# Second normalisation of a conv and graph-attention block: four slices of variances on rows of their own

## The chip, the cores and the metric

The kernel runs on one core of a Trainium2 chip. The metric is the device time of one launch in microseconds; lower is better.

## What is computed

The input x is 16 images of 64 channels, 56 x 56 pixels, in f32. The reference does, cut to what matters:

```
x = x + conv3x3(bfp8(_ln_c(x)), bfp8(weight)) + bias     # _ln_c: over channels
t = tokens of x                                          # 16*3136 tokens of 64 channels
t = t + ffn(_ln_t(t))        # _ln_t: (t - mean) / sqrt(var + 1e-5), over the 64 channels
# ffn: h = t @ W_gat (16 numbers a token); graph attention over 262144 edges + loops;
#      the sums choose 2 of 4 experts per token; each expert is 64 -> 128 -> gelu -> 64
```

The change lies in `_ln_t`, the second normalisation.

## The kernel before, in words

The program has three phases, one behind the other, with a barrier between them.

The first phase counts and ranks the edges, normalises x the first time, quantises it, convolves it, normalises the sum the second time (`D`, the tokens) and projects the tokens. Beside that it sorts the edges: 32 groups of edges (`SG`) each give a table `run_slots`, which GpSimd scatters to memory with 17 indirect DMAs a group (line 470, 544 in all). The second phase gathers node rows by edge, 16 gathers a step (line 1097), adds up the attention sums and runs the experts. The third phase weighs and adds the experts' outputs.

There is no scheduler: each engine has its own program, in the order written, and waits on semaphores.

An image lies in SBUF as 128 partitions (two halves of the rows, 64 channels each) by 4 chunks of 392 pixels. A loop over image pairs (`image_pair`) handles image `b` on each engine as follows.

- VectorE: one-hot tables for the sort (lines 837, 839), the sum of convolution and input (line 972), `spread_step` (844), the rest of the one-hots, the centring `D = X - mean` (981), one more `spread_step`, then the reciprocal of `std2` (986), the product `D * rstd` (988) and the places of the group (851 to 860).
- ScalarE: squares of `D` into `S` (707), the root of the variances into `std2` (709), the copy of the sort's sums into `run_slots` (`group_out`, 669), the copy of the projected rows (701).
- TensorE: the mean (`mean_of`, 530), half a sort step (16 matmuls, 582), the variances (637), half a sort step, the spreading of the reciprocals (643), half a sort step, then, once line 988 is done, the convolution of the next image (614), half a sort step and the projection (623).
- GpSimd: the 17 scatters of a group, once `slots` (860) and `run_slots` (669) of that group are there. The two buffers of `run_slots` are filled again when their scatters have landed.
- SyncE: loads of images, stores of `X`, `D` and `rows`, and at the end waits for all stores.

The variances: for chunk `c` a 128 x 32 matrix `thin` (1/64 in column 0 for the upper half's channels, in column 1 for the lower half's) is the stationary operand, the 392 squares of the chunk are moved, and the result lies in rows 32c and 32c+1 of PSUM tile `A`, 392 columns wide. Root and reciprocal work on 128 x 392, though two rows in 32 hold something. `fan` (32 rows of a chunk by 128) then spreads each chunk's two rows over 64 partitions each.

In the compiled program an f32 matmul is two pairs of a weight load and a matmul (two passes), standing one behind the other; the profile counts both. The four matmuls of line 637 write four column strips of 32 of the array (`128*32` in the profile); the four of line 643 read four row strips of 32 (`32*128`).

Of the kernel before, what the change touches and what calls it, by code (L numbers as in the profile page):

```python
# [11 lines left out]
ALU = mybir.AluOpType  # L12
ACT = mybir.ActivationFunctionType
AX = mybir.AxisListType

P = 128


B, CH, HGT, WID = 16, 64, 56, 56
# [3 lines left out]
CHUNK = HALF // CHUNKS  # L23
# [18 lines left out]
FLAT_P = GROUPS_P * GROUP  # L42
assert QCHUNKS * QGROUPS == GROUPS_P
QUAD = P // CHUNKS
MAGIC = 1.5 * 2.0 ** 23
TINY = 2.0 ** -100
EXP_BITS = 0x7F800000
# [75 lines left out]
def link(eng, instr, sig):  # L123

    instr.then_inc(sig.sem, 1)
    sig.k += 1
    eng.wait_ge(sig.sem, sig.value)
# [19 lines left out]
def build(nc, x, conv_w, conv_b, w_gat, att_src, att_dst, b_gat, ln_g, ln_b, w1, b1, w2, b2, edges, out):  # L147
    ctx = ExitStack()
    with ctx:
        def sb(name, shape, dt=F32):  # L150
            return ctx.enter_context(nc.sbuf_tensor(name, shape, dt))
# [31 lines left out]
        eps_t = sb("eps_t", [P, 1])  # L183
# [11 lines left out]
        b2s = sb("b2s", [P, EXPERTS])  # L195
        pick = sb("pick", [2 * 3 * EXPERTS, EXPERTS, P], BF16)
        fold = sb("fold", [P, CH])
        thin = sb("thin", [P, QUAD])
        fan = sb("fan", [P, P])

        A = ctx.enter_context(nc.psum_tensor("A", [P, 4, 512], F32))
        C = ctx.enter_context(nc.psum_tensor("C", [P, 4, 512], F32))

        with ExitStack() as ph:
            def tb(name, shape, dt=F32):
                return ph.enter_context(nc.sbuf_tensor(name, shape, dt))
# [12 lines left out]
                t.append(edge_t[:].bitcast(F32)[:, 0:HALF].rearrange("p (c n) -> p c n", c=CHUNKS))  # L219
            S = tb("S", [P, CHUNKS, CHUNK])  # L220
            Q = [tb(f"Q{k}", [P, HALF_ROWS + 2, WID + 2], BF16) for k in range(2)]
            std2 = tb("std2", [P, CHUNK])
            dev = tb("dev", [TOK, TOK_TILES, 2])
            rstd = tb("rstd", [TOK, TOK_TILES, 2])
            rows = tb("rows", [TOK, TOK_TILES, 2 * ROW])
# [180 lines left out]
            def _(pool):  # L406
                step = Signal(s["pstep"])
                link(pool, pool.memset(tally[:], 0.0), step)
                for r in range(2):
# [3 lines left out]
                                              pattern=[[-1, P]], channel_multiplier=1), step)  # L413
# [3 lines left out]
                for r in range(2):  # L417
                    link(pool, pool.affine_select(out=fold[:], in_=fold[:], compare_op=ALU.not_equal, fill=1.0, base=-r * CH,
                                                  pattern=[[-1, CH]], channel_multiplier=1), step)
# [3 lines left out]
                                              pattern=[[-1, P]], channel_multiplier=1), step)  # L423
# [6 lines left out]
                for h in range(2):  # L430
                    link(pool, pool.memset(halves[h * CH:(h + 1) * CH, h * CH:(h + 1) * CH], 1.0 / CH), step)
                link(pool, pool.memset(thin[:], 0.0), step)
                for h in range(2):
                    link(pool, pool.memset(thin[h * CH:(h + 1) * CH, h:h + 1], 1.0 / CH), step)
                link(pool, pool.memset(fan[:], 0.0), step)
                for c in range(CHUNKS):
                    for h in range(2):
                        link(pool, pool.affine_select(out=fan[:, h * CH:(h + 1) * CH], in_=fan[:, h * CH:(h + 1) * CH], compare_op=ALU.not_equal, fill=1.0,
                                                      base=-(c * QUAD + h), pattern=[[0, CH]], channel_multiplier=1), step)
                link(pool, pool.memset(eps_c[:], 1e-6), step)  # L440
                link(pool, pool.memset(eps_t[:], 1e-5), step)
                for k in range(2):
# [9 lines left out]
                for h in range(2):  # L452
                    mine = pick[:, :, h * CH:(h + 1) * CH]
                    for r in range(3):
                        link(pool, pool.affine_select(out=mine, in_=mine, compare_op=ALU.not_equal, fill=1.0, base=-(h * 3 + r) * EXPERTS,
                                                      pattern=[[-1, EXPERTS], [0, CH]], channel_multiplier=1), step)
                pool.memset(scratch_i[:], 0).then_inc(s["const_ready"], 1)

                n = PLACES * RUN * FIELDS // 8
# [92 lines left out]
            def _(pe):  # L552
                pe.wait_ge(s["rank_const"], 2)
                for b in range(NB):
                    pe.wait_ge(s["masks_ready"], b + 1)
                    for c in range(4):
                        mm = pe.matmul(C[:, c, :], tally[:, TWIN - 1 - b:TWIN - 1 - b + P], mask_h[:, b % 2, c * PSUM_COLS:(c + 1) * PSUM_COLS],
                                       start=(b == 0), stop=(b == NB - 1))
# [4 lines left out]
                n = NB * SG // 4  # L563
# [63 lines left out]
                def image_pair(i, last=False):  # L627
                    for k in range(2):
                        b, g = i * 2 + k, i * 2 + k + SG // 2 + 1
                        sorts = not (last and k == 1)  # L630
                        pe.wait_ge(s["summed"], b + 1)
                        mean_of(pe, X[k], s["mean2_ready"])
                        if sorts:
                            sort_step(g, 1 - k, 0, 0)
                        pe.wait_ge(s["squared2"], b + 1)
                        for c in range(CHUNKS):
                            mm = pe.matmul(A[c * QUAD:(c + 1) * QUAD, 0, 0:CHUNK], thin[:], S[:, c, :], start=True, stop=True)
                        mm.then_inc(s["var2_ready"], 1)
                        if sorts:
                            sort_step(g, 1 - k, 0, 1)  # L640
                        pe.wait_ge(s["rstd2_ready"], b + 1)
                        for c in range(CHUNKS):
                            mm = pe.matmul(A[:, c, 0:CHUNK], fan[c * QUAD:(c + 1) * QUAD, :], std2[c * QUAD:(c + 1) * QUAD, :], start=True, stop=True)
                        mm.then_inc(s["rstd2_spread"], 1)
                        if sorts:
                            sort_step(g, 1 - k, 1, 0)
                        pe.wait_ge(s["tokens_ready"], b + 1)
                        if sorts:
                            convolve(i + k, 1 - k)
                            sort_step(g, 1 - k, 1, 1)  # L650
                        project(b, k)
# [6 lines left out]
            @block.scalar  # L658
            def _(act):
                act.wait_ge(s["const_ready"], 1)  # L660
                act.wait_ge(s["blocks_ready"], 1)
                act.dma_start(blk_d.rearrange("(p k) -> p k", p=P), unit_blk_i[:]).then_inc(s["blk_stored"], 16)

                def group_out(i, k):

                    act.wait_ge(s["step_sums"], i * 4 + k * 2 + 2)
                    if not (isinstance(i, int) and i == 0):
                        act.wait_ge(sent[k], i * (RUN_COLS * 16))
                    act.copy(run_slots[:, k].rearrange("p c v -> p v c"),  # L669
                             C[:, k, 0:FIELDS * SLOT_COLS].rearrange("p (v c) -> p v c", v=FIELDS)).then_inc(s["group_out"], 1)  # L670

                def deviations(eps, k, ready):
                    act.activation(dev[:].rearrange("p j h -> p (j h)"), C[0:TOK, k, VAR_AT:VAR_AT + 2 * TOK_TILES], ACT.Sqrt, bias=eps[0:TOK]).then_inc(ready, 1)

                def part_squares(u):
                    b, k, cs, part = part_of(u)
                    act.wait_ge(s["centred"], u + 1)
                    act.activation(S[:, cs], D[k][:, cs], ACT.Square).then_inc(s["squared"], 1)

                def part_deviations(u):  # L680
                    b, k, cs, part = part_of(u)
                    act.wait_ge(s["var_ready"], u + 1)
                    act.activation(dev1[:, part].rearrange("p j h -> p (j h)"), A[0:PTOK, cs.start, CHUNK:CHUNK + 2 * PTOK_TILES], ACT.Sqrt,
                                   bias=eps_c[0:PTOK]).then_inc(s["deviated"], 1)

                part_squares(0)
                for u in range(UNITS):
                    part_deviations(u)
                    if u + 1 < UNITS:
                        part_squares(u + 1)  # L690
                for k in range(2):
                    group_out(0, k)
                with act.Fori(1, SG // 4) as i:
                    for k in range(2):
                        group_out(i, k)
                group_out(SG // 4, 0)
                def rows_out(b):
                    act.wait_ge(s["projected"], b + 1)
                    if not (isinstance(b, int) and b == 0):
                        act.wait_ge(s["rows_stored"], b * 32)  # L700
                    act.copy(rows[:].rearrange("p (k j) f -> p k (j f)", k=2), C[0:TOK, 2:4, 0:14 * ROW]).then_inc(s["rows_ready"], 1)

                def image_pair(i, last=False):
                    for k in range(2):
                        b = i * 2 + k
                        act.wait_ge(s["centred2"], b + 1)
                        act.activation(S[:], D[k], ACT.Square).then_inc(s["squared2"], 1)
                        act.wait_ge(s["var2_ready"], b + 1)
                        act.activation(std2[:], A[:, 0, 0:CHUNK], ACT.Sqrt, bias=eps_t[:]).then_inc(s["deviated2"], 1)
                        if not (last and k == 1):  # L710
                            group_out(i + SG // 4 + k, 1 - k)
                        rows_out(b)
                image_pair(0)
                with act.Fori(1, B // 2 - 1) as i:
                    image_pair(i)
                image_pair(B // 2 - 1, True)

            @block.vector
# [958 lines left out]
```

## Time and profile before

| what | value |
|---|---|
| median of three runs | 4388.38 us (4383.29 to 4395.43) |
| the profiled execution | 4386.45 us, its span 4384.7 us |
| VectorE busy | 2789.1 us, 64% |
| GpSimd busy | 2963.9 us, 68% |
| TensorE busy | 3496.4 us, 80%; granted clock 0.806 on average |
| ScalarE busy | 1013.6 us, 23% |

The first phase lies at 0 to about 1291 us of the span, the second at 1292 to about 4064, the third behind it. The images of the second normalisation come at 870 to 1287 us. A row of the profile names the line, the engine, the tiles written and read and the time; in brackets stand the idle time before it and who ended it.

### The profile page before, as it was taken

How to read it: one execution, taken by the hardware profiler on the slowest of the kernel's cores; microseconds unless marked ns; L12 is line 12 of the kernel's file. 1: busy time of each engine (PE TensorE's matmuls, PEld its weight loads, DVE VectorE, ACT ScalarE, POOL GpSimd, SP SyncE). 2: the span in 40 equal slices, each digit the busy share in tenths (PEclk: the TensorE clock that was granted, in tenths of full speed). 3: DMA queues.
4: the chain of work that ended last, by engine and by line, in shares of the span. 5: the costliest groups of instructions: out<-in, count | busy, mean ns of one | idle time of the engine just before them, and what ended most of it. 6: DMA issues, size and time to landing. Idle time of an engine off the chain costs nothing. (4 is left out here: it accounts for less than half of the span.)

```text
span 4384.7 us, 60136 instructions
## 1 busy us (share of the span) xinstructions
PE 3496.4 (80%) x19024; PEld 2414.3 (55%) x19025; DVE 2789.1 (64%) x3513; ACT 1013.6 (23%) x1820; POOL 2963.9 (68%) x2936
## 2 busy tenths in 40 slices
PE   4786333488853999999999999999999999986064
PEld 1454323355543766676676667666666666666010
DVE  8788999888864455455455545554545454545977
ACT  0110000011111333333333333333333333320100
POOL 3000788887757777777777777777777777776088
PEclk8898555688875899889889988988988898887555
DMA  1243111399989222222222222222222222221299
GB/s 51 60 103 84 43 48 48 48 116 115 122 114 86 37 38 34 37 37 37 33 37 37 34 36 37 37 33 33 37 34 36 33 37 36 35 27 10 93 301 340
DMA packets 357672, 284.59 MB, mean 65 GB/s; under 512 B 253586, under 2 KB 329938, under 8 KB 357204
## 3 DMA queue, kind: packets, MB, share of 16 engines
q1 hardware_dynamic: 245620, 199.65, 22.1%
q0 software_dynamic: 87552, 29.20, 7.2%
q10 hardware_dynamic: 24416, 54.71, 6.0%
q8 instruction: 42, 0.69, 0.1%
q14 instruction: 42, 0.34, 0.0%
HBM read 161.06 MB, written 122.27 MB: 65 GB/s over the span
## 5 line engine op out<-in xcount | busy, mean ns | idle before, releaser
L1097 POOL DMA_INDIRECT gath<-tab_d,src_no x2116 | 1996.6, 944 | 644.9 <-issue 644.9
L470 POOL DMA_INDIRECT edge_d<-run_slots,slots x544 | 672.9, 1237 | 569.4 <-ACT run_slots L669 406.6
L1401 DVE TENSOR_TENSOR acc<-acc,C 128x160 f32 x1090 | 349.8, 321 | 1043.8 <-PE C L1228 930.9
L1228 PEld LDWEIGHTS C<-spread,lo_hot 128*128 128x128 f32 x4360 | 776.9, 236 | 257.9 <-issue 194.7
L1228 PE MATMUL C<-spread,lo_hot 128*128 128x160 f32 x4360 | 846.4, 360 | 72.9 <-DVE spread L1389 71.0
L1212 PEld LDWEIGHTS C<-damp,lo_hot_t 128*128 128x128 f32 x4384 | 558.6, 207 | 85.6 <-issue 85.6
L1212 PE MATMUL C<-damp,lo_hot_t 128*128 x4384 | 575.5, 288 | 5.8 <-ACT lo_hot_t L1125 5.8
L1139 ACT ACTIVATE mlp<-A,b2s 64x392 f32<-64x392 f32 x512 | 298.0, 582 | 1068.8 <-PE A L1247 1068.8
L1237 PE MATMUL A<-T,w1s 64*128 64x392 f32 x1024 | 525.7, 596 | 23.4 <-DMA T<-t_d 23.4
L582 PE MATMUL C<-wide_rec,hot_lo 128*128 128x136 f16 x2048 | 271.7, 305 | 298.0 <-DVE wide_rec L844 298.0
L1247 PE MATMUL A<-hid,w2s 128*64 128x392 f32 x1024 | 451.8, 523 | 0.0
L582 PEld LDWEIGHTS C<-wide_rec,hot_lo 128*128 128x128 f16 x2048 | 241.8, 123 | 350.1 <-DVE wide_rec L844 292.0
L1130 ACT ACTIVATE hid<-A,b1s 128x392 f32<-128x392 f32 x512 | 300.6, 587 | 483.7 <-PE A L1237 483.6
L1389 DVE TENSOR_TENSOR spread<-hi_hot,C 128x2560 f32<-128x2560 f32 x137 | 386.4, 2820 | 4.7
L1125 ACT COPY lo_hot_t<-A 128x512 f32<-128x512 f32 x548 | 292.8, 588 | 235.7 <-PE A L1202 235.7
L1202 PEld LDWEIGHTS A<-ident,lo_hot 128*128 128x128 f32 x2192 | 241.3, 143 | 192.2 <-issue 192.1
L1202 PE MATMUL A<-ident,lo_hot 128*128 128x128 f32 x2192 | 303.3, 282 | 41.0 <-PE A L1237 35.3
L1329 DVE TENSOR_TENSOR lo_hot<-C,lo 128x2048 f32<-128x2048 f32 x137 | 314.0, 2292 | 16.3
L1237 PEld LDWEIGHTS A<-T,w1s 64*128 64x128 f32 x1024 | 165.1, 201 | 268.9 <-issue 238.7
L669 ACT CAST run_slots<-C 128x136 f16<-128x136 f32 x32 | 10.0, 312 | 677.4 <-PE C L582 615.6
L1379 DVE TENSOR_TENSOR C<-gath,C 128x64 f32<-128x64 f32 x137 | 31.3, 229 | 210.9 <-DMA gath<-tab_d,src_no 184.8
L1576 POOL TENSOR_TENSOR four<-pairs 128x392 f32<-128x392 f32 x64 | 79.1, 1235 | 127.6 <-DVE pairs L1654 126.3
(272 smaller groups left out, 3247.0 us busy)
## 6 DMA issues: line engine op xcount, KB each, us to landing
mlp_d<-mlp ACTq DMA_DIRECT2D x128, 392.0 KB
mlp<-mlp_d SPq DMA_DIRECT2D x64, 784.0 KB, 6.5
gath<-tab_d,src_no POOLq DMA_INDIRECT x2116
pixels<-in_x SPq DMA_DIRECT2D x32, 392.0 KB, 6.4
src<-in_x SPq DMA_DIRECT2D x32, 392.0 KB, 6.5
T<-t_d SPq DMA_DIRECT2D x128, 98.0 KB
X<-x_d SPq DMA_DIRECT2D x64, 196.0 KB, 8.4
out<-X SPq DMA_DIRECT2D x128, 98.0 KB, 6.8
```

The lines of the kernel that those rows point to most:

```text
L470: pool.indirect_dma_start(edge_d, bass.IndirectOffsetOnAxis(ap=slots[:, k, c:c + 1], axis=0), run_slots[:, k, c * RUN:(c + 1) * RUN, :].re ...
L582: mm = pe.matmul(C[:, k, 0:FIELDS * SLOT_COLS], hot_lo[:, j, t // LINE, :, t % LINE], fields[:, t // LINE, :, t % LINE], start=(j == 0 and ...
L1097: pool.indirect_dma_start(gath[:, g % BUFS, j, :], None, node_d if g < BUFS else tab_d, bass.IndirectOffsetOnAxis(ap=src_no[:, t:t + 1], a ...
L1130: act.activation(hid[:], A[:, 2, 0:CHUNK], ACT.Gelu, bias=b1s[:, e:e + 1]).then_inc(s["gelu_ready"], 1)
L1202: mm = pe.transpose(A[:, j // 4, (j % 4) * P:(j % 4 + 1) * P], lo_hot[:, k, half * G // 2 + j, :], ident[:])
L1212: mm = pe.matmul(C[:, 0, t * HI * HEADS:(t + 1) * HI * HEADS], lo_hot_t[:, t, :], damp[:, bass.ds(qs[t // U - half * UG // 2], HI), :].rea ...
L1228: mm = pe.matmul(C[:, bank, at:at + HI * VALS], lo_hot[:, k % UNROLL, u * U + j, :], spread[:, u * U + j].rearrange("p h v -> p (h v)"), s ...
L1237: pe.matmul(A[:, 2, 0:CHUNK], w1s[a, e, :], T[a, :], start=True, stop=True).then_inc(s["hidden"], 1)
L1247: pe.matmul(A[h * CH:(h + 1) * CH, 3, 0:CHUNK], w2s[:, e, :], hid[:], start=True, stop=True).then_inc(s["expert_done"], 1)
L1329: dve.tensor_tensor(lo_hot[:, k], lane_v.rearrange("p (k h) -> p k h", k=1).broadcast_to([P, G, P]), lo[:, bass.ds(g * G, G)].rearrange("p ...
L1389: dve.tensor_tensor(spread[:], hi_hot[:, k].rearrange("p t (h k) -> p t h k", k=1).broadcast_to([P, G, HI, VALS]), vals.rearrange("p t (k ...
L1401: L(dve.tensor_tensor(here, here, C[:, bank, at:at + HI * VALS].rearrange("p (h v) -> p h v", h=HI), ALU.add))
```

## The change

A chunk's 392 pixels are cut into four slices of 98. The variances of slice n go to rows 32c + 2n and 32c + 2n + 1, so all four slices of a chunk share the same 98 columns, and `std2` is 128 x 98. For that `thin` and `fan` have four versions, one a slice; each of the four matmuls of line 637 becomes four that add into the same 32 x 98 of PSUM (the columns of `thin` that aren't slice n's are zero), and each of the four of line 643 becomes four of 98 columns.

```
-        thin = sb("thin", [P, QUAD])
-        fan = sb("fan", [P, P])
+        thin = sb("thin", [P, SLICES, QUAD])
+        fan = sb("fan", [P, SLICES, P])
...
-            std2 = tb("std2", [P, CHUNK])
+            std2 = tb("std2", [P, SLICE])
...
-                for h in range(2):
-                    link(pool, pool.memset(thin[h * CH:(h + 1) * CH, h:h + 1], 1.0 / CH), step)
+                for n in range(SLICES):
+                    for h in range(2):
+                        link(pool, pool.memset(thin[h * CH:(h + 1) * CH, n, 2 * n + h:2 * n + h + 1], 1.0 / CH), step)
                 link(pool, pool.memset(fan[:], 0.0), step)
                 for c in range(CHUNKS):
                     for h in range(2):
-                        link(pool, pool.affine_select(out=fan[:, h * CH:(h + 1) * CH], in_=fan[:, h * CH:(h + 1) * CH], compare_op=ALU.not_equal, fill=1.0,
-                                                      base=-(c * QUAD + h), pattern=[[0, CH]], channel_multiplier=1), step)
+                        mine = fan[:, :, h * CH:(h + 1) * CH]
+                        link(pool, pool.affine_select(out=mine, in_=mine, compare_op=ALU.not_equal, fill=1.0,
+                                                      base=-(c * QUAD + h), pattern=[[-2, SLICES], [0, CH]], channel_multiplier=1), step)
...
                         for c in range(CHUNKS):
-                            mm = pe.matmul(A[c * QUAD:(c + 1) * QUAD, 0, 0:CHUNK], thin[:], S[:, c, :], start=True, stop=True)
+                            for n in range(SLICES):
+                                mm = pe.matmul(A[c * QUAD:(c + 1) * QUAD, 0, 0:SLICE], thin[:, n, :], S[:, c, n * SLICE:(n + 1) * SLICE],
+                                               start=(n == 0), stop=(n == SLICES - 1))
...
                         for c in range(CHUNKS):
-                            mm = pe.matmul(A[:, c, 0:CHUNK], fan[c * QUAD:(c + 1) * QUAD, :], std2[c * QUAD:(c + 1) * QUAD, :], start=True, stop=True)
+                            for n in range(SLICES):
+                                mm = pe.matmul(A[:, c, n * SLICE:(n + 1) * SLICE], fan[c * QUAD:(c + 1) * QUAD, n, :], std2[c * QUAD:(c + 1) * QUAD, :],
+                                               start=True, stop=True)
...
-                        act.activation(std2[:], A[:, 0, 0:CHUNK], ACT.Sqrt, bias=eps_t[:]).then_inc(s["deviated2"], 1)
+                        act.activation(std2[:], A[:, 0, 0:SLICE], ACT.Sqrt, bias=eps_t[:]).then_inc(s["deviated2"], 1)
```

## Rows read from the trace of the kernel before

**Rows 1.** Groups of GpSimd at 1310 to 4060 us: busy, mean ns, idle before and releasers

```profile
L1097 POOL DMA_INDIRECT gath<-tab_d,src_no x2116 | 1996.6, 944 | 644.9 <-issue 644.9
```

**Rows 2.** Groups of GpSimd at 902 to 1252 us

```profile
L470 POOL DMA_INDIRECT edge_d<-run_slots,slots x230 | 281.2, 1223 | 70.1 <-issue 68.0 <-ACT run_slots L669 1.8 <-DVE slots L860 0.3
```

**Rows 3.** Timeline of the end of the first phase: start us, us, instruction, [idle before]

```profile
1261.68 0.96 POOL L470 DMA_INDIRECT edge_d<-run_slots,slots  x1 [0.31 <-issue]
1263.84 0.31 ACT L669 CAST run_slots<-C 128x136 f16<-128x136 f32 x1 [14.80 <-PE C L582]
1264.94 0.96 POOL L470 DMA_INDIRECT edge_d<-run_slots,slots  x1 [2.30 <-ACT run_slots L669]
...
1285.13 0.96 POOL L470 DMA_INDIRECT edge_d<-run_slots,slots  x1 [0.31 <-issue]
1285.94 0.72 ACT L701 COPY rows<-C 112x672 f32<-112x672 f32 x1 [11.79 <-PE C L623]
1286.75 1.11 SPq L377 DMA_DIRECT2D node_d<-rows  x2
...
1292.04 1.11 SPq L1068 DMA_DIRECT2D lo_hot<-edge_d  x2
```

**Rows 4.** Waits of SyncE's queue at 1280 to 1300 us: total, times, longest

```profile
SPq L401 <- DMA node_d<-rows: 3.2, 1, 3.2
```

**Rows 5.** Timeline of one image's normalisation, from the squares to the convolution

```profile
1032.58 1.51 ACT L707 ACTIVATE S<-pixels 128x1568 f32<-128x1568 f32 x1 [4.26 <-DVE pixels L981]
1033.90 2.50 DVE L844 TENSOR_TENSOR wide_rec<-flat_count,rec 128x2176 f16<-128x2176 f16 x2 [0.16 <-DVE flat_count L839]
1034.14 0.96 PE L637 MATMUL A<-S,thin 128*32 128x392 f32 x8 [1.95 <-ACT S L707]
1035.04 2.19 PE L582 MATMUL C<-wide_rec,hot_lo 128*128 128x136 f16 x16
1035.15 0.59 ACT L709 ACTIVATE std<-A,eps_t 128x392 f32<-128x392 f32 x1 [1.06 <-PE A L637]
1036.31 2.60 DVE L986 RECIPROCAL std<-std 128x392 f32<-128x392 f32 x1
1038.96 1.69 PE L643 MATMUL A<-std,fan 32*128 32x392 f32 x8 [1.74 <-DVE std L986]
1040.72 1.79 DVE L988 TENSOR_TENSOR pixels<-pixels,A 128x1568 f32<-128x1568 f32 x1 [1.81 <-PE A L643]
```

**Rows 6.** Groups of VectorE at 902 to 1252 us

```profile
L986 DVE RECIPROCAL std<-std 128x392 f32<-128x392 f32 x14 | 36.4, 2600 | 0.1
L988 DVE TENSOR_TENSOR dst<-dst,A 128x1568 f32<-128x1568 f32 x7 | 12.5, 1789 | 11.2 <-PE A L643 11.2
L988 DVE TENSOR_TENSOR pixels<-pixels,A 128x1568 f32<-128x1568 f32 x6 | 10.7, 1788 | 10.1 <-PE A L643 10.1
```

**Rows 7.** Smaller operations of the same kinds, from the groups by form

```profile
L915 DVE RECIPROCAL rstd<-dev 98x16 f32<-98x16 f32 x32 | 7.9, 246 | 5.2 <-ACT dev L683 5.2
L683 ACT ACTIVATE dev<-A,eps_c 98x16 f32<-98x16 f32 x32 | 8.8, 274 | 235.9 <-PE A L496 235.9
```

**Rows 8.** TensorE started by 1007.75 us, and the granted clock (next to last group) in four bursts

```profile
1007.70 0.88 PE L637 MATMUL A<-S,thin 128*32 128x392 f32 x4 [2.09 <-ACT S L707]
...
1034.09:1035.10 1.01, 0.96 (x9) 0.23 (x10) 1.01 (x1) 0.00 (x0) 0.70 (x2) 0.84 1.37 208
1038.90:1040.70 1.80, 1.74 (x9) 0.63 (x10) 0.01 (x1) 0.00 (x0) 1.50 (x2) 0.50 0.04 2
1007.65:1009.30 1.65, 1.60 (x10) 0.34 (x11) 1.65 (x2) 0.00 (x0) 1.35 (x2) 0.50 1.28 257
1012.50:1013.60 1.10, 1.01 (x10) 0.46 (x11) 0.04 (x2) 0.00 (x0) 0.88 (x1) 1.00 0.03 2
```

**Rows 9.** Timeline of TensorE: f32 bursts in column strips and on the whole array

```profile
204.28 1.57 PE L507 MATMUL A<-ident,rstd 98*64 98x98 f32 x32
...
1024.61 2.88 PE L623 MATMUL C<-proj,dst 128*112 128x48 f32 x28
```

**Rows 10.** Timeline of the constants: GpSimd, then VectorE's masks beside them and alone

```profile
2.90 0.62 POOL L418 TENSOR_SCALAR_AFFINE_SELECT fold<-fold 128x64 f32<-128x64 f32 x2
7.73 8.56 POOL L438 TENSOR_SCALAR_AFFINE_SELECT fan<-fan 128x64 f32<-128x64 f32 x8
17.50 6.30 DVE L742 TENSOR_SCALAR mask_h<-blk_h 128x2048 bf16<-128x2048 bf16 x4
35.79 0.71 POOL L457 MEMSET scratch_i<- 128x128 int32 x1
53.04 0.69 DVE L742 TENSOR_SCALAR mask_h<-blk_h 128x2048 bf16<-128x2048 bf16 x1 [0.23 <-PE C L557]
68.55 2.29 DVE L746 TENSOR_REDUCE group_tot<-C 128x32 f32<-128x2048 f32 x1 [1.13 <-PE C L557]
```

More of the change, by code:

```diff
@@ L44 @@
 QUAD = P // CHUNKS
+SLICES = 4
+SLICE = CHUNK // SLICES
+assert SLICE * SLICES == CHUNK and 2 * SLICES <= QUAD
 MAGIC = 1.5 * 2.0 ** 23
```

## The prediction, made before the changed kernel ran

> **What bounds the kernel now.** I read the page's slices first, then the groups of GpSimd by stage, then the timeline of one image and of the end of the first phase.
>
> The second phase is GpSimd's: 2116 gathers are busy 1996.6 us and sit idle 644.9 us for nothing but their own issue [rows 1]. It starts when the first phase ends, so what the change does to the end of the first phase reaches the total one for one, and nothing else of it does.
>
> In the stage that the change touches, GpSimd is full too. In 350 us it made 230 scatters, 281.2 us busy and 68.0 us issue; it waited 2.1 us for others [rows 2]. So 17 scatters, a group, take 350 / 230 x 17 = 25.9 us. A lone scatter takes 0.96 us and 0.30 to issue [rows 3], 21.4 us a group; the other 4 us are scatters that last longer than 0.96 us (the mean is 1.22) and that come whatever the reciprocal does.
>
> VectorE keeps nearly the same pace beside it: there is almost no idle time but 21.3 us in 13 images ahead of line 988, waiting for line 643 [rows 6]. So two chains run side by side. How they end is in [rows 3]: GpSimd's scatter of 1261.68 ends at 1262.64, and the last group's first waits for ScalarE's copy until 1264.94, that is 2.0 us beyond its normal 0.30. Its seventeenth ends at 1286.09. The image chain ends with the rows' copy at 1286.66 and their store at 1286.75; SyncE waits 3.2 us for that store alone [rows 4], and issues the next phase's first load at 1292.04. SyncE came to that wait from the one on GpSimd's block at about 1288.0 (1291.2 less 3.2, where 1291.2 is the end of the wait as I read it, 0.8 us ahead of the next phase), so the scatters had landed 3.9 us before the rows' store at most (at 1287.3 if a scatter lands 1.2 us behind its row).
>
> **The change, part by part.** *The reciprocal.* 16 columns take 246 ns [rows 7] and 392 take 2600 [rows 6]: 6.26 ns a column, so 98 take 246 + 82 x 6.26 = 759 ns. It saves 1.84 us an image, 29.4 us over 16. *The root.* 274 ns at 16 columns [rows 7], 590 at 392 [rows 5]: 98 take 343, 0.25 us saved, on the chain only if the root is late.
>
> *The matmuls.* Columns moved stay the same, instructions go from 8 to 32 passes a burst. What a pass of 98 columns costs is in line 507: 32 passes in two column strips side by side, 1.57 us with about 0.22 of tail, so 16 after one another in a strip, 84 ns each [rows 9]; the loads of 64 columns are covered. Line 623 shows a pass that its weight load bounds: 28 in 2.88 us, 103 ns for 112 columns [rows 9]; the new `fan` passes load 128, so I take 103 x 128 / 112 = 118 ns. Both at the clock's upper level; at the lower one twice that.
>
> How many passes lie side by side is what decides. Before, line 637 had four of its eight passes started within 50 ns (x4) [rows 8], though in the program the second pass of strip 0 stands ahead of the first of strip 1. So TensorE lets a strip's instructions wait and starts those behind them for another strip, at least 6 instructions further on (second load and pass of three strips). For full overlap it has to reach past 14 waiting ones of each of three strips, 42. The trace shows no such reach, nor that it fails.
> - Full overlap: 8 passes deep, 0.67 us and 0.94 us, with tails of about 0.2: T1 = 0.9, T2 = 1.15, sum 2.05; at the lower clock 3.8 us.
> - No overlap: 32 x 84 ns = 2.7 and 32 x 118 = 3.8, with tails 6.9 us; at the lower clock 13.
> - A reach of 4 to 8 instructions a strip: the next strip starts when 5 (or 3) passes of this one have run, 3 x 5 + 8 = 23 (or 17) deep: 1.9 + 2.7 + 0.4 = 5.0 (or 3.8) us; lower clock twice.
>
> The Trainium skill, "TensorE: Matmul & The Clock Gate", section on packing small matmuls, says that matmuls start and end strictly in program order. By it the first strip's eight passes would run ahead of the second's, the row "no overlap". The x4 row speaks against it in its strict form.
>
> *What these cost the image.* The squares end at 1034.09 and line 988 starts at 1040.72, 6.6 us later; VectorE is free for the reciprocal 2.25 us after the squares, then 2.6 and 1.64 us of mean wait (21.3 / 13) give 6.5 as the mean [rows 5, 6]. Afterwards TensorE sets it: T1, half a sort step 2.17 us that stands between the bursts, T2, and 0.25 us of hand-overs; the reciprocal is done before. So line 988 comes at T1 + T2 + 2.4, and the **break-even is T1 + T2 = 4.1 us**. VectorE's spare time isn't lost otherwise: the convolution follows 988, and conv, sort half, projection and mean stand in the same order as before. So d = 4.1 - (T1 + T2) is gained, or lost, an image.
>
> *What reaches the end.* A gain ends where GpSimd does: the 3.9 us by which it was ahead, and the 2.0 us that its last group waited, 5.9 us. 16 d reaches that at d = 0.37, so T1 + T2 = 3.75 is enough, which full overlap gives even at the lower clock. A loss has no such cover: ScalarE's copy of the last group comes 15 d later, the last rows 16 d. Line 637 and 643 together saw both clock levels (0.50, 0.50, 0.84, 1.00) [rows 8].
>
> *Constants.* Eight `affine_select` of 256 columns for 64: 0.24 us in line 418 [rows 10], I estimate 0.14 more each, 1.1 us; six more small memsets and two wider ones 1.3 us. They end at 36.5 us, VectorE needs them at 68 [rows 10]: 30 us of cover. But VectorE's masks take 6.30 / 4 = 1.58 us beside GpSimd's work and 0.69 + 0.23 alone [rows 10], so 2.4 us more of it cost up to 2.4 x 0.42 = 1.0 us ahead of everything. Between 0 and 1.0 I take 0.5. If GpSimd slows as in line 438 (0.94 us a select for 0.24), this could be three times as much.
>
> **The sum.** -5.9 + 0.5 = -5.4 us for full overlap: the profiled execution goes from 4386.45 to 4381.05; the median of the runs is 1.93 above it, so 4388.4 - 5.4 = **4383 us**. 0.3% of this kernel, 13 us, is what a measurement can tell from no change.
>
> **Rivals.**
> - *A, the forecast*: overlap deep enough, GpSimd bounds. 4383, own range 4377 to 4391. For it: strips overlap already, and the cap makes the result insensitive. 47%.
> - *B, strips one after another (ends slower)*: line 637 and 643 fill one strip's queue and the others stand idle. Place: the two bursts between squares and line 988; d = 4.1 - 6.9 = -2.8, x 16 = 45 us, 4433; nearer 4480 with half of it at the lower clock. It decides from T1 + T2 above 4.9 (13 us). For it: all passes of a strip now follow one another. Against it: the x4 row. 20%. The rule of the Trainium skill's "TensorE: Matmul & The Clock Gate" would give this rival.
> - *C, a short reach*: 3.8 to 5.0 us at the upper clock, half as much again with mixed clocks, 5.7 to 7.5: d from +0.3 to -3.4, times between 4384 and 4440, the middle 4405. 28%, of which a quarter stays within 13 us of before.
> - *D, all of the reciprocal reaches the end*: 4388 - 29 = 4359. It needs GpSimd to get faster by 25 us, which the 2.1 us of waits exclude unless its long scatters shrink. 3%.
> - *E, the change is lost in something else*, such as more instructions to fetch, within 13 us: 2%.
>
> Faster by over 0.3%: D, 3%. Same: A, a quarter of C, E: 56%. Slower: the rest of C and B, 41%. The range goes from 4376 to 4432: left out are D, and of B and C what mixed clocks make longer, some 17%.
>
> **What would show it.** Line 986 at 0.76 us and line 709 at 0.34. Line 637 and 643 with 32 passes each in 0.9 and 1.2 us (A), in 2 and 2.7 (C), 2.7 and 3.8 (B). In A the wait ahead of GpSimd's last group is gone and SyncE's last wait is for the scatters; in B and C line 988 waits 3 us and more, and the last group's wait grows by 15 d. The prediction is wrong if TensorE's reach is short, or if the longer bursts run at the lower clock where the reach is middling.

## The result, and the profile after

The changed kernel takes 4414.05 us (median of 5 runs, 4404.73 to 4420.42) where the kernel before takes 4393.65 us (median of 5 runs, the three of the table above among them). The ratio is 1.0048, 95% interval 1.0029 to 1.0067: slower, by 13 to 29 us. Forecast was 5.4 us less than before. Three single runs in this document (one of the kernel before, two of later experiments) took 4630 to 5496 us at a granted clock of 0.58 to 0.72 over the whole run, and are left out of every median, count and ratio below. The profiled execution took 4407.87 us, its span is 4406.1 us, 21.4 us more than before's.

The small operations are as forecast. Groups of VectorE in the stage of the images (busy us, mean ns, idle time ahead and who ended it), to be read beside [rows 6]:

```profile
L997 DVE TENSOR_TENSOR pixels<-pixels,A 128x1568 f32<-128x1568 f32 x8 | 14.3, 1788 | 29.7 <-PE A L651 29.7
L997 DVE TENSOR_TENSOR dst<-dst,A 128x1568 f32<-128x1568 f32 x7 | 12.5, 1787 | 25.2 <-PE A L651 25.2
L995 DVE RECIPROCAL std<-std 128x98 f32<-128x98 f32 x16 | 12.3, 767 | 6.3 <-ACT std L718 4.8
```

The reciprocal (now line 995) fell from 2600 to 767 ns; 759 was forecast. But the product behind it (988 before, 997 now) waits (29.7 + 25.2) / 15 = 3.66 us for TensorE's spreading matmuls, where it waited 21.3 / 13 = 1.64 us. One image shows why; this is the stretch of [rows 5] in the new kernel:

```profile
1012.41 1.51 ACT L716 ACTIVATE S<-dst 128x1568 f32<-128x1568 f32 x1 [3.79 <-DVE dst L990]
1013.74 2.49 DVE L853 TENSOR_TENSOR wide_rec<-flat_count,rec 128x2176 f16<-128x2176 f16 x2 [0.16 <-DVE flat_count L848]
1013.97 1.97 PE L643 MATMUL A<-S,thin 128*32 128x98 f32 x32 [1.49 <-ACT S L716]
1015.88 2.16 PE L587 MATMUL C<-wide_rec,hot_lo 128*128 128x136 f16 x16
1015.99 0.34 ACT L718 ACTIVATE std<-A,eps_t 128x98 f32<-128x98 f32 x1 [2.06 <-PE A L643]
1016.36 0.77 DVE L995 RECIPROCAL std<-std 128x98 f32<-128x98 f32 x1
1017.97 2.72 PE L651 MATMUL A<-std,fan 32*128 32x98 f32 x32
1020.73 1.79 DVE L997 TENSOR_TENSOR dst<-dst,A 128x1568 f32<-128x1568 f32 x1 [3.60 <-PE A L651]
```

The variances (now line 643) take 1.97 us and the spreading (now 651) 2.72 us, both at the clock's upper level:

```profile
1013.90:1015.95 2.05, 1.98 (x33) 1.83 (x34) 2.05 (x2) 0.02 (x1) 1.66 (x2) 1.00 1.23 275
1017.90:1020.70 2.80, 2.80 (x35) 2.63 (x34) 0.00 (x0) 0.00 (x0) 2.19 (x3) 1.00 0.05 3
```

(Windows: stretch, length, then busy time of TensorE, its weight load, VectorE, ScalarE, GpSimd, then the granted clock, here 1.00, the share of the DMA engines and GB/s.) So the reciprocal is done at 1017.13, 0.8 us before TensorE comes out of its half sort step and can use it, and the 2.72 us behind it are all on the path. The sum of the two bursts is 4.69 us against the break-even of 4.1.

The end of the first phase, as in [rows 3]:

```profile
1278.09 0.31 ACT L678 CAST run_slots<-C 128x136 f16<-128x136 f32 x1 [16.07 <-PE C L587]
1279.20 0.96 POOL L475 DMA_INDIRECT edge_d<-run_slots,slots  x1 [3.06 <-ACT run_slots L678]
...
1300.87 0.72 ACT L710 COPY rows<-C 112x672 f32<-112x672 f32 x1 [11.63 <-PE C L628]
1301.68 1.10 SPq L380 DMA_DIRECT2D node_d<-rows  x2
1306.95 1.10 SPq L1077 DMA_DIRECT2D lo_hot<-edge_d  x2
```

The wait ahead of GpSimd's last group did not go, it grew from 2.30 to 3.06 us. GpSimd's waits for `run_slots` over the whole stage (total us, times, longest) show more, first before and then after the change:

```profile
POOL edge_d L470 <- ACT run_slots L669: 4.4, 8, 2.3
```

```profile
POOL edge_d L475 <- ACT run_slots L678: 12.0, 11, 3.1
```

So GpSimd, which was nearly always busy or issuing before, is now held up by the image chain ahead of several of its last groups. The next phase starts at 1306.95 instead of 1292.04, 14.9 us later. The images themselves begin 3.1 us later. Here is the first convolution in each kernel, before and after:

```profile
852.28 2.14 PE L614 MATMUL A<-Q,cw_t 128*128 128x392 bf16 x6 [2.62 <-DMA pixels<-in_x]
```

```profile
855.42 1.81 PE L619 MATMUL A<-Q,cw_t 128*128 128x392 bf16 x5 [3.65 <-DMA pixels<-in_x]
```

From there to the store of the last rows it is 1286.75 - 852.28 = 434.5 us before and 1301.68 - 855.42 = 446.3 after: **the image chain is 11.8 us longer**. The rest of the 21.4 us is 3.1 us ahead of it, and 6.5 us in the second and third phases, where the kernels are the same: their gathers end 5.4 us further apart (2737.0 us from the first gather to the last, 2731.6 before). A second execution of the changed kernel, below, did not repeat those 5.4 us.

### The profile page after: what moved, and what is told of

It is laid out like the page before. It is cut to its first block and busy times, and to the rows that moved or that the text cites. A ratio compares the mean times of both kernels' runs of the same rounds, so it can differ in the third digit from the quotient of the medians.

```text
span 4406.1 us, 61678 instructions
## 1 busy us (share of the span) xinstructions
PE 3545.6 (80%) x19792; PEld 2481.7 (56%) x19793; DVE 2760.7 (63%) x3513; ACT 1011.5 (23%) x1820; POOL 2973.6 (67%) x2942
```

## The experiments

Two measures are used beside the ratio. **Chain** is the time from the first convolution to the store of the last rows (to the second of its two transfers, so it is 0.3 us more than the differences above); **stage** that from GpSimd's first scatter to its first gather. I used these because the time of the first scatter itself lay between 439.9 and 456.2 us over the executions, the kernel before among them at 445.6; the two executions of the changed kernel had it at 447.5 and 456.2. **T1 and T2** are the mean bursts of variances and spreading: the busy time of the group over the 16 images, divided by 16; they mix images at both levels of the clock. All columns but the ratio are of one execution each.

| kernel | T1 + T2, us | chain | stage | ratio to before, 95% interval |
|---|---|---|---|---|
| before | 1.27 + 1.46 = 2.73 | 434.8 | 869.5 | |
| after | 1.98 + 2.82 = 4.80 | 446.6 | 882.6 | 1.0048 (1.0029 to 1.0067) |
| after, once more | 2.17 + 2.88 = 5.05 | 450.4 | 885.5 | 1.0040 (1.0023 to 1.0057) |
| strips in turn, both bursts | 1.40 + 1.61 = 3.01 | 412.2 | 863.3 | 0.9977 (0.9964 to 0.9990) |
| strips two by two | 1.49 + 1.61 = 3.10 | 413.2 | 863.8 | 0.9981 (0.9964 to 0.9999) |
| two slices | 1.28 + 1.44 = 2.72 | 418.7 | 865.3 | 0.9995 (0.9983 to 1.0006) |
| variances in turn only | 1.16 + 4.12 = 5.28 | 451.4 | 887.6 | 1.0043 (1.0027 to 1.0058) |
| spreading in turn only | 2.93 + 1.16 = 4.09 | 430.0 | 866.9 | 0.9999 (0.9987 to 1.0012) |
| before, short reciprocal | 1.38 + 1.32 = 2.70 | 415.0 | 862.7 | 0.9973 (0.9958 to 0.9987) |
| before, new constants | 1.28 + 1.55 = 2.83 | 436.3 | 870.8 | 1.0004 (0.9993 to 1.0014) |

**The strips in turn.** The only edit on the changed kernel is the order of its two loops, so that one after another the strips get a matmul each; instructions, sizes and constants are the same.

```
-                        for c in range(CHUNKS):
-                            for n in range(SLICES):
+                        for n in range(SLICES):
+                            for c in range(CHUNKS):
```

(The same four lines in line 641 for the variances and in 649 for the spreading.)

> The changed kernel with the slice loop outside and the chunk loop inside in both bursts, so that neighbouring matmuls go to different strips of the array; nothing else differs. Theory S (a strip holds about 5 waiting instructions, then the instructions for other strips are not reached): order is what made the bursts long. Expected: line 643 about 0.9 us and line 651 about 1.2 us from start to end, in place of 1.97 and 2.7; line 997 no longer waits on TensorE for 3.6 us but about 1.5; the wait ahead of GpSimd's last group (3.06 us after the change) is gone, first phase about 20 us shorter than after the change, 5 us shorter than before. Total about 4386 against 4391 before (the constants' 2 us counted). Rival O (each instruction has a price of its own, 60 ns a matmul whatever its strip): the bursts stay at 1.9 and 2.6 us and the time stays at 4410.

It took 4378.02 us (12 runs) against 4388.57 (35 runs), ratio 0.9977 (0.9964 to 0.9990): faster than both kernels. The forecast of 0.9 and 1.2 us holds at the upper level of the clock, as rows further down show; the means are 1.40 and 1.61 us because some of the bursts ran at the lower level. Groups of TensorE at 850 to 1320 us, first the changed kernel, then this one:

```profile
L651 PE MATMUL A<-std,fan 32*128 32x98 f32 x512 | 45.1, 286 | 1.2 <-DVE std L995 1.2
L643 PE MATMUL A<-S,thin 128*32 128x98 f32 x512 | 31.6, 250 | 26.4 <-ACT S L716 26.4
```

```profile
L651 PE MATMUL A<-std,fan 32*128 32x98 f32 x512 | 25.7, 357 | 1.2 <-DVE std L995 1.2
L643 PE MATMUL A<-S,thin 128*32 128x98 f32 x512 | 22.4, 345 | 38.1 <-ACT S L716 38.1
```

The same 2 x 512 passes cost 76.7 us in one order and 48.1 in the other. Note the mean of a single pass, which goes the other way (286 to 357, 250 to 345 ns): passes of four strips that run side by side each last longer. The number to read is the busy time of the group.

How the strips start is seen by asking for TensorE's variance burst up to a moment, and counting. In the changed kernel, up to 1014.32 and up to 1014.35 us:

```profile
1013.97 0.53 PE L643 MATMUL A<-S,thin 128*32 128x98 f32 x4 [1.49 <-ACT S L716]
1013.97 0.64 PE L643 MATMUL A<-S,thin 128*32 128x98 f32 x6 [1.49 <-ACT S L716]
```

For 350 ns only four passes start; then two more within 30 ns. The rows don't name the strip. I read them as four passes of the first strip, then its fifth and the first of the second strip: the first strip's passes follow one another at some 90 ns, and the pair fits that spacing only as one more of them and a newcomer. The length fits too: three such delays of 0.37 us and the 0.89 us that a burst takes whose four strips start together make 2.0 us, and 1.97 were measured. The same question to the kernel with the strips in turn, up to 1022.94, and then the whole burst's row:

```profile
1022.89 0.29 PE L643 MATMUL A<-S,thin 128*32 128x98 f32 x4 [2.16 <-ACT S L716]
...
1022.89 1.38 PE L643 MATMUL A<-S,thin 128*32 128x98 f32 x32 [2.16 <-ACT S L716]
```

Four passes within 50 ns, as before the change [rows 8]. In that program order the second pass of a strip stands ahead of the next strip's first one, so what waits lets others by. But a strip has room for three waiting passes only, as the next experiments bear out: while one runs and three wait, a fifth holds up all that stands behind it.

The clock does not explain the difference. The spreading burst took 2.72 us at a granted clock of 1.00 in the changed kernel; here it took 2.04 at 0.50:

```profile
1000.25 2.04 PE L651 MATMUL A<-std,fan 32*128 32x98 f32 x32
```

```profile
1000.20:1002.30 2.10, 2.10 (x34) 1.88 (x34) 0.00 (x0) 0.00 (x0) 1.79 (x2) 0.50 0.68 40
```

The end of the phase shows what limits it now. Timeline of the same kernel:

```profile
1260.46 0.72 ACT L710 COPY rows<-C 112x672 f32<-112x672 f32 x1 [10.31 <-PE C L628]
1261.27 1.10 SPq L380 DMA_DIRECT2D node_d<-rows  x2
...
1274.91 0.96 POOL L475 DMA_INDIRECT edge_d<-run_slots,slots  x1 [0.30 <-issue]
1280.68 1.10 SPq L1077 DMA_DIRECT2D lo_hot<-edge_d  x2
```

The image chain is 22.6 us shorter than before, and ends 13.6 us ahead of GpSimd's last scatter. The stage gains 6.2 us.

**The reciprocal alone.** The kernel before, with its reciprocal on 98 of 392 columns.

```
-                        dve.reciprocal(std2[:], std2[:]).then_inc(s["rstd2_ready"], 1)
+                        dve.reciprocal(std2[:, 0:98], std2[:, 0:98]).then_inc(s["rstd2_ready"], 1)
```

> The kernel before, with the reciprocal taken of 98 of the 392 columns only; the other columns of std2 keep the root, so later values are wrong. TensorE's bursts are as before. It shows what the saved VectorE time is worth. Theory G (GpSimd's scatters bound the stage): 29 us of VectorE are saved and 3 to 6 us reach the end, 4386 against 4391. Rival V (VectorE bounds the stage): 25 us or more reach the end, 4365.

4376.2 us (10 runs), ratio 0.9973 (0.9958 to 0.9987), that is 6 to 18 us faster; the stage is 6.8 us shorter and the chain 19.8. So 29 us less of VectorE's time are worth some 20 us to the chain and 7 to the stage. The expectation was 3 to 6 us; 6.8 us in the stage is just above it, and far from rival V's 25. This is what the change could have brought, and the kernel with the strips in turn brings it.

**Two slices.** The changed kernel with `SLICES = 2`, 128 x 196 and four passes of a strip in a row, in the order of the change.

```
-SLICES = 4
+SLICES = 2
```

> The changed kernel with two slices of 196 columns in place of four of 98, chunk loop still outside. A strip then gets four passes in a row, eight instructions: two run, one load goes ahead, five wait. Theory S (a strip holds about five waiting instructions): the other strips start within 50 ns, line 643 takes about 0.9 us and line 651 about 1.0 us as before the change. With a reciprocal of 1.37 us the stage ends with GpSimd, total about 4386. If fewer than five are held: line 643 about 1.4 us, total about 4391. Rival O (a price an instruction of 60 ns a matmul): 16 passes, about 1.0 and 1.3 us too, so the two are told apart by the start times of the strips, not by the total.

4387.3 us (10 runs), ratio 0.9995 (0.9983 to 1.0006). Groups of TensorE at 850 to 1320 us:

```profile
L651 PE MATMUL A<-std,fan 32*128 32x196 f32 x256 | 23.0, 487 | 5.1 <-DVE std L995 5.1
L643 PE MATMUL A<-S,thin 128*32 128x196 f32 x256 | 20.4, 446 | 39.2 <-ACT S L716 39.2
```

23.0 and 20.4 us, the bursts of before (23.3 and 20.4) to a per cent. The start times, by which the expectation wanted to tell the theories apart, agree. Up to 64 ns after the burst's start all four strips have begun:

```profile
1006.55 0.40 PE L643 MATMUL A<-S,thin 128*32 128x196 f32 x4 [2.45 <-ACT S L716]
```

With four passes of a strip, one runs and three wait, and the next strip isn't held up. Stage and chain (4.2 and 16.1 us shorter) agree with that; the time over all runs shows less than the stage does.

**The constants alone.** The kernel before builds the four versions of `thin` and `fan` and uses the first.

```
-        thin = sb("thin", [P, QUAD])
-        fan = sb("fan", [P, P])
+        thin4 = sb("thin4", [P, 4, QUAD])
+        fan4 = sb("fan4", [P, 4, P])
...
-                            mm = pe.matmul(A[c * QUAD:(c + 1) * QUAD, 0, 0:CHUNK], thin[:], S[:, c, :], start=True, stop=True)
+                            mm = pe.matmul(A[c * QUAD:(c + 1) * QUAD, 0, 0:CHUNK], thin4[:, 0, :], S[:, c, :], start=True, stop=True)
```

> The kernel before, with the four versions of thin and fan built as in the changed kernel and version 0 used in the old matmuls; std2, root, reciprocal and matmuls are as before (the fan version has the same two rows a chunk). It prices the constants alone. Theory: GpSimd's work of about 2 to 4 us more at the start slows VectorE's masks beside it; the first scatter comes 1 to 2 us later, 447.5 against 445.7, and nothing else changes: total +2 us. Rival: the move of every later tile in SBUF, or something else in the second phase, makes the +5 us seen there: then +7 us in total.

4390.39 us (12 runs), ratio 1.0004 (0.9993 to 1.0014). Nothing that can be measured: the prediction's 0.5 us and the 2 us expected here lie inside the interval (3 us less to 6 more), the rival's 7 us just outside.

**The change once more.** The changed kernel, beside the next two.

> The changed kernel once more, beside the two below on one chip, because only 13 of its 20 us lay between the first scatter and the first gather of the two profiled executions. Theory: the stage costs 13 us and the rest was the scatter of executions, ratio 1.003. Rival: something outside the stage costs another 5 us or more, ratio 1.005 again.

4404.39 us (7 runs) against 4386.89 (18 runs), ratio 1.0040 (1.0023 to 1.0057). The interval holds 1.003 as well as 1.005, so the times don't decide between theory and rival; the profile does in part. The chain took 450.4 us, the stage 885.5, the gathers 2731.8: the second phase's 5.4 us were of that one execution, and the stage alone cost 16.0.

**One burst in turn at a time.** The edit of the loops in line 641 alone, then in line 649 alone.

> The changed kernel with the slice loop outside in the variance burst (line 643) only; the spreading burst (line 651) keeps its order. Theory S (a strip holds three waiting passes): line 643 takes 0.9 us at the upper clock and 1.4 at the lower, line 651 stays at 2.7 us, sum 3.6 to 4.1 against a break-even of 4.1: the stage ends like before the change, total 0 to -5 us against before. Rival (the spreading burst alone matters, since the variance burst is covered by VectorE's own work): no better than the changed kernel, +13 us.

> The changed kernel with the slice loop outside in the spreading burst (line 651) only; the variance burst (line 643) keeps its order. Theory S: line 643 stays at 1.97 us, line 651 takes 1.2 us at the upper clock and 2.0 at the lower, sum 3.2 to 4.0, the stage ends with GpSimd: total -3 to -6 us against before. Rival (the variance burst alone matters): +13 us as after the change.

Variances alone: 4405.15 us (6 runs), ratio 1.0043 (1.0027 to 1.0058), as slow as the change. Spreading alone: 4386.28 us (11 runs), ratio 0.9999 (0.9987 to 1.0012), the time of before. Both were expected a few microseconds below before, and the first missed by far; its rival named the right time. Groups of TensorE, first of the one, then of the other:

```profile
L651 PE MATMUL A<-std,fan 32*128 32x98 f32 x512 | 66.0, 374 | 1.2 <-DVE std L995 1.2
L643 PE MATMUL A<-S,thin 128*32 128x98 f32 x512 | 18.5, 300 | 30.4 <-ACT S L716 30.4
```

```profile
L643 PE MATMUL A<-S,thin 128*32 128x98 f32 x512 | 46.9, 329 | 41.1 <-ACT S L716 41.1
L651 PE MATMUL A<-std,fan 32*128 32x98 f32 x512 | 18.5, 281 | 1.2 <-DVE std L995 1.2
```

Each edit shortens its own burst, to 1.16 us. In both, the burst that was left as it was became longer, from 2.82 to 4.12 and from 1.98 to 2.93 us. In the first kernel the clock stands beside it: timeline and window of one image,

```profile
1016.45 0.89 PE L643 MATMUL A<-S,thin 128*32 128x98 f32 x32 [1.56 <-ACT S L716]
...
1019.44 4.95 PE L651 MATMUL A<-std,fan 32*128 32x98 f32 x32
```

```profile
1019.40:1024.30 4.90, 4.90 (x33) 4.70 (x32) 0.00 (x0) 0.00 (x0) 3.68 (x5) 0.50 0.24 19
```

4.95 us at a granted clock of 0.50, 2.72 at 1.00. Ten of the 16 spreading bursts of this kernel took so long. The lower level stretches either order by about the same factor (2.04 us with the strips in turn above, 1.15 at the upper level, below), but it adds 2.2 us to the long burst and 0.9 to the short one. The burst with the strips in turn at the upper level, in the second kernel:

```profile
1006.47 1.15 PE L651 MATMUL A<-std,fan 32*128 32x98 f32 x32
```

```profile
1006.40:1007.60 1.20, 1.20 (x35) 1.04 (x34) 0.00 (x0) 0.00 (x0) 0.95 (x1) 1.00 0.03 2
```

That the kernel with one burst mended is no faster than the change is so explained: the sum of its bursts is 5.28 us, more than the 4.80 of the change.

The second kernel tests the break-even itself. Its bursts sum to 4.09 us, where 4.1 was the forecast's point of no change, and the chain took 430.0 us against 434.8, the time 0.9999. It also answers the rival that the spreading burst alone counts: that burst is shorter here (1.16 us) than in the kernel with both in turn (1.61), yet the chain gained 4.8 us and not 22.6. The variance burst, 2.93 against 1.40 us, makes the difference.

**Two by two.** If a strip has room for three waiting passes, then two slices of a strip may stand in a row (four passes), and the order need not go strip by strip.

```
-                        for c in range(CHUNKS):
-                            for n in range(SLICES):
+                        for c, n in [(c, m + j) for m in (0, 2) for c in range(CHUNKS) for j in range(2)]:
```

> The changed kernel with both bursts in the order strip 0 slices 0 and 1, strip 1 slices 0 and 1, and so on, then slices 2 and 3 of each strip: four passes in a row a strip, twice. The sums are the same. Theory S (each strip has room for three waiting passes of its own, whatever the others hold): all four strips start within 50 ns, the fifth to eighth passes are fed as room comes, a strip's fifth pass comes at most one pass late; line 643 at the upper clock about 0.9 to 1.0 us, line 651 about 1.2 to 1.4, and the stage ends with GpSimd, -3 to -6 us against before. Rival W (one common window of about five waiting instructions): strips start one after another as after the change, bursts near 2 and 2.7 us, +13 us.

4381.71 us (10 runs) against 4392.32 (13 runs), ratio 0.9981 (0.9964 to 0.9999). TensorE's variance burst, up to 58 ns after its start and whole:

```profile
869.91 0.32 PE L642 MATMUL A<-S,thin 128*32 128x98 f32 x4 [1.50 <-ACT S L714]
...
869.91 0.93 PE L642 MATMUL A<-S,thin 128*32 128x98 f32 x32 [1.50 <-ACT S L714]
```

All four strips start at once, 0.93 us in all. Ahead of the fourth strip's first pass stand nine waiting passes, three in each of three strips; in the order of the change the passes of the first strip alone held up the second. So the room belongs to each strip and is not one shared queue. Here the order stands in the kernel's own text: strip 0's matmul of slice 1 is written ahead of strip 1's first, and strip 1 doesn't wait for it.

**GpSimd out of the way.** Twelve of 17 scatters a group, in the kernel before, in the one with the strips in turn and in the changed one. Five a group are left out, so edges are missing in the output.

```
-                        for c in range(RUN_COLS):
+                        for c in range(12):
...
-                    pool.wait_ge(sent[k], SG // 2 * RUN_COLS * 16)
+                    pool.wait_ge(sent[k], SG // 2 * 12 * 16)
```

> The kernel before with 12 of the 17 scatters of each group; 5 are left out, so edges are missing in the output. It takes GpSimd out of the stage (12 x 1.26 = 15 us a group instead of 26). Theory G (image chain and GpSimd end the stage together): the image chain is left and ends as before or up to 5 us earlier, since no scatter delays it; total 4383 to 4389. The second phase does the same gathers.

> The changed kernel with the slice loop outside in both bursts and 12 of the 17 scatters a group. The image chain of the interleaved kernel was 22 us shorter than before from the first convolution to the last rows' store, while the stage as a whole gained 6. Theory G (GpSimd absorbs the rest): without GpSimd's bound the whole of it reaches the end, 16 to 22 us less than the kernel before with 12 scatters. Rival: only 6 us, if the chain's end is set by something else, such as the loads of the images.

> The changed kernel with 12 of the 17 scatters a group. Theory: TensorE's bursts set the image chain, GpSimd does not matter for the loss: 12 to 14 us more than the kernel before with 12 scatters. Rival: a part of the loss comes from GpSimd's scatters meeting VectorE's work at other moments; then less than 8 us is left.

| with 12 scatters (4 runs each) | median, us | ratio to before with all 17 (4383.04 us, 7 runs) | stage | chain |
|---|---|---|---|---|
| before | 4458.42 | 1.0175 (1.0152 to 1.0199) | 861.9 | 430.7 |
| strips in turn | 4431.41 | 1.0113 (1.0094 to 1.0131) | 837.8 | 407.6 |
| after | 4468.7 | 1.0193 (1.0176 to 1.0210) | 875.7 | 445.6 |

All three are slower than with 17, and the 4383 to 4389 us expected of the first was missed: the time behind the first gather is 65 to 82 us longer. The places that no edge was scattered to are the likely reason, but no run shows it. The three are to be compared with each other. Strips in turn against before: 24.1 us less in the stage and 27.0 in the time, where it was 6.2 with all scatters. So GpSimd swallows 24.1 - 6.2 = 18 us of the gain. After against before: 13.8 us more in the stage (13.1 and 16.0 with all scatters), 10.3 in the time. GpSimd covers a gain and no loss, and the loss doesn't come through it.

## Why the prediction was wrong

*The step that failed is "How many passes lie side by side".* It took full overlap, 42 waiting instructions past, for the value and gave 0.9 and 1.15 us. Measured are 1.98 and 2.82 us (means), and 1.97 and 2.72 in an image at the upper clock. The text had the other case beside it, rival C, "a reach of 4 to 8 instructions a strip", 17 to 23 passes deep, 1.9 + 2.7 us and the tails. That is what the chip did: the next strip starts with the fifth pass of this one, so the last strip starts after 3 x 4 = 12 and the burst is 12 + 8 = 20 passes deep, 20 x 84 ns = 1.7 us and 0.2 of tail. The row x4 [rows 8] spoke against strict order, and I let it speak for full overlap as well; it showed one waiting pass a strip and no more. With the 4.1 us of break-even, C at the upper clock gives d = 4.1 - 4.8 = -0.7 us an image, 11.2 us over 16: the chain grew by 11.8. Shown: the same instructions in another order, and in the same order with four passes a strip, take 3.0 and 2.7 us and lose nothing. The prices of a pass were about right: with the strips in turn at the upper level the bursts took the 0.9 and 1.15 us of full overlap. The measured 4414 us lies inside the stated range only because the range took in rival C, with 4405 as its middle.

*Strict program order* (the Trainium skill, "TensorE: Matmul & The Clock Gate", section on packing small matmuls), rival B, would have given 2.7 and 3.8 us. Neither came at the upper clock, and with the strips in turn four passes start within 50 ns. For passes of different strips the measurement decides against the rule, up to three waiting passes a strip.

*The reciprocal and the root* were right: 767 for 759 ns, 0.34 for 343 ns. *The constants* too: no cost that can be measured.

*What these cost the image* was right. The break-even of 4.1 us stood the test of a kernel that has 4.09 to about 0.3 us an image: its chain gained 4.8 us over 16 images. In the changed kernel's image shown above, line 997 starts 6.81 us after the squares end, 2.1 us more than the two bursts, where the prediction had 2.4; that would put the break-even at 4.4. Gains and losses of the chain by 16 x (4.1 - T1 - T2) against those measured:

| kernel | worked out, us | measured, us |
|---|---|---|
| after | -11 | -11.8 |
| after, once more | -15 | -15.6 |
| variances in turn | -19 | -16.6 |
| spreading in turn | 0 | +4.8 |
| strips in turn | +17 | +22.6 |
| two by two | +16 | +21.6 |
| two slices | +22 | +16.1 |

Within 6 us everywhere, and in the right order but for the last row, where the rule takes the reciprocal to be done in time: at 196 columns it takes 1.37 us, nearly twice as long as with four slices, and line 651 waits 5.1 us for it.

*What reaches the end.* That GpSimd caps a gain was right: the stage gained 5.7 to 6.8 us when the chain gained 20 to 23, and with fewer scatters all of it came through. That the cap's 5.9 us fit so well is partly luck. With the strips in turn the last group's extra wait of 2.0 us went, as forecast. But the next phase's first load came 4.8 us after the last scatter's end, against 5.95 before, so GpSimd's lead was worth 1.1 us and not 3.9. The rest is that the 544 scatters were busy 669.3 us in place of 672.9, which the prediction put at nothing; over all the runs with 17 scatters that sum lies between 669 and 678 us, so it may be chance. That rival D, the whole reciprocal, is not to be had is shown with it. A loss has no cover, as the text said: chain +11.8, stage +13.1; again +15.6 and +16.0. It didn't come as one wait of 15 d (some 10 us) ahead of the last group, though, but spread over several groups: 12.0 us of waits in all, against 4.4 before.

*Still open.* The time over all runs grew by 20.4 us in the first comparison and 17.5 in the second, the stage by 13.1 and 16.0. The difference of 2 to 7 us is no more than the half width of the intervals (7 to 8 us), and I found no stage that has it in both executions. The gains show it too: with the strips in turn the time fell by 10.6 us and the stage by 6.2.

## What to carry to other kernels

When matmuls on separate strips of the array are to run side by side, write them so that the strips take turns; a long row of passes for one strip holds up the others as surely as a wait. Count passes and not matmuls (an f32 matmul is two), and count them again whenever a burst is cut into smaller ones with the same number of columns. Before making an operation shorter, work out for each engine beside it how much of the gain it lets through: here 29 us less on VectorE were worth 6 to 7 in the stage, while bursts longer by 2 us an image on TensorE took that gain and 13 to 16 us more, and nothing covered it.

## What the runs showed of the hardware

- A strip has room for three passes that wait. In the variance burst of 98 columns the next strip starts only with the fifth pass of this one, some 0.37 us after the first. With at most three waiting in each strip all four start within 50 to 64 ns. Each pass had a weight load of its own, so the runs don't tell whether the room is counted in passes or in instructions.
- 32 passes of 98 columns took 0.89 us (variances) and 1.15 us (spreading) with the strips in turn at the upper level of the clock, 1.97 and 2.72 us strip by strip. At the lower level the spreading took 2.04 us with the strips in turn and 4.95 strip by strip.
- Granted clock of the stage. The mean over the images was 0.84 before, with TensorE busy 343 of 405 us, and 0.93 after, with 387 of 415:

```profile
875.00:1290.00 415.00, 387.46 (x3019) 296.43 (x3016) 321.47 (x282) 45.21 (x62) 325.31 (x266) 0.93 0.93 112
```

  So the change was slower at a higher clock. With one burst shortened the other fell to the lower level in the image that is shown above, which I had not expected: mending one of two bursts can take from the other what it gives.
